# Order of the up/gate loop in a fused attention and gated feed-forward layer: weight block outermost instead of token block outermost

## What is computed

```python
def _L0_ffn_ref(x, w_gate, w_up, w_down):      # w_* are int32, scaled by 1/127
    gate = jnp.einsum('bsd,hd->bsh', x, wg)
    up = jnp.einsum('bsd,hd->bsh', x, wu)
    h = jax.nn.silu(gate) * up
    return jnp.einsum('bsh,dh->bsd', h, wd)

x = L0_attn_x                                  # (4, 4096, 1024) float32
x = x + _layernorm(_L0_attn_ref(_layernorm(x), W_spin, b_spin, W_global, W_J, beta))
x = x + _layernorm(_L0_ffn_ref(_layernorm(x), w_gate, w_up, w_down))
```

## Time and profile before

| what | value |
| --- | --- |
| median of 2 runs | 1491.61 us (1490.85 to 1492.37) |
| the profiled execution, its own time | 1483.44 us |
| its span on the slowest core (core 3) | 1480.8 us |
| spans of the 8 cores | 1467.2 to 1480.8 us |
| share of the span in which TensorE was busy | 81% |
| bytes read from and written to HBM | 167.81 MB, 25.17 MB |

### The profile page before, as it was taken

One profiled execution on the slowest core, in us unless ns is written; L12 is line 12 of the kernel. 1 busy time (PEld: TensorE's weight loads), 2 busy tenths in 40 slices (PEclk: granted clock), 3 DMA queues, 4 the chain that ended last, 5 costly groups with the idle time before them and its releaser, 6 DMA issues.

```text
span 1480.2 us, 14639 instructions; the slowest of 8 cores (1467.2 to 1480.8 us)
## 1 busy us (share of the span) xinstructions
PE 1201.1 (81%) x5274; PEld 512.8 (35%) x5274; DVE 376.8 (25%) x608; ACT 217.8 (15%) x338; POOL 200.6 (14%) x236
## 2 busy tenths in 40 slices
PE   0888887699999999999960777787787666699997
PEld 0233332234444444444420333333333222244443
DVE  2243344101121121121124322332332111123443
ACT  0111112111122122122120111111112100000000
POOL 0011110000000000000010333333343433200000
PEclk9999999999999999999985898999999988899999
DMA  9756557551223233223129999999999999923332
GB/s 191 141 137 134 119 139 192 96 97 43 50 53 72 48 56 72 45 58 72 36 69 251 113 166 169 144 182 163 143 159 146 148 120 131 146 62 114 91 109 85
DMA packets 380150, 168.77 MB, mean 114 GB/s; under 512 B 354480, under 2 KB 354480, under 8 KB 380080
## 3 DMA queue, kind: packets, MB, share of 16 engines
q0 software_dynamic: 207504, 67.13, 43.5%
q1 hardware_dynamic: 102688, 79.74, 22.0%
q10 hardware_dynamic: 69888, 20.98, 7.2%
HBM read 167.81 MB, written 25.17 MB: 130 GB/s over the span
## 4 chain that ended last, share of the span: by engine, by line
PE 64%; DMA 27%; DVE 3%; issue 2%; POOL 1%; ACT 1%; SPq 1%; ACTq 1%; DVEq 0%; POOLq 0%
DMA wu_sb<-wuT 19%; PE ps_q L544 15%; PE ps_pv L651 15%; PE ps_d L1102 11%; PE ps_s L257 6%; PE ps_g L955 6%; DMA xnT_sb<-xn_bf 5%; PE ps_u L967 5%; PE ps_e L306 3%; DMA xs<-x 1%; PE ps_s L253 1%; POOL wg_sb L932 1%; DMA xn2T<-xn_bf 1%; PE ps_pv L428 1%; DMA x_sc<-x_buf 1%
## 5 line engine op out<-in xcount | busy, mean ns | idle before, releaser
L955 PE MATMUL ps_g<-xn2T,wg_sb 128*128 128x512 bf16 x768 | 196.4, 402 | 179.1 <-DMA wu_sb<-wuT 122.7
L544 PE MATMUL ps_q<-s_FM,ebuf 128*128 128x512 bf16 x1024 | 226.6, 382 | 9.0 <-DMA ebuf<-e_sc 9.0
L651 PE MATMUL ps_pv<-s_tok,PT_sb 128*128 128x512 bf16 x1024 | 225.3, 381 | 0.9 <-DVE g_bc L494 0.9
L932 POOL DMA_DIRECT2D wg_sb<-wgT x96 | 84.6, 881 | 802.0 <-DMA attn_sc<-attn_wb 477.9
L967 PE MATMUL ps_u<-xn2T,wu_sb 128*128 128x512 bf16 x768 | 187.3, 388 | 0.0
L955 PEld LDWEIGHTS ps_g<-xn2T,wg_sb 128*128 128x128 bf16 x768 | 74.2, 101 | 290.4 <-issue 219.0
L1102 PE MATMUL ps_d<-wdT_sb,h_act 128*128 128x512 bf16 x768 | 165.9, 379 | 1.1 <-DVE h_act L990 1.1
L990 DVE SCALAR_TENSOR_TENSOR h_act<-silu_b,ps_u 128x512 bf16<-128x512 f32 x96 | 65.2, 686 | 332.2 <-PE ps_u L967 308.1
L544 PEld LDWEIGHTS ps_q<-s_FM,ebuf 128*128 128x128 bf16 x1024 | 100.3, 98 | 132.6 <-issue 14.0
L651 PEld LDWEIGHTS ps_pv<-s_tok,PT_sb 128*128 128x128 bf16 x1024 | 100.7, 98 | 122.9 <-issue 3.4
L257 PE MATMUL ps_s<-wspT_sb,xnT_sb 128*128 128x512 bf16 x512 | 135.0, 411 | 0.0
(11 more groups left out here) (67 smaller groups left out, 436.6 us busy)
## 6 DMA issues: line engine op xcount, KB each, us to landing
xs<-x SPq DMA_DIRECT2D x24, 1024.0 KB, 6.4
wg_sb<-wgT POOLq DMA_DIRECT2D x96, 256.0 KB, 9.5
wu_sb<-wuT POOLq DMA_DIRECT2D x96, 256.0 KB, 13.1
x_sc<-x_buf SPq DMA_DIRECT2D x16, 512.0 KB, 8.0
xs<-x_sc SPq DMA_DIRECT2D x16, 512.0 KB, 4.5
out<-out_b SPq DMA_DIRECT2D x16, 512.0 KB, 5.3
wdT_sb<-wdT POOLq DMA_DIRECT2D x4, 1536.0 KB, 19.6
e_sc<-e_stage POOLq DMA_DIRECT2D x32, 128.0 KB, 2.4
```

Of the source, the lines that this page charges most:

```text
L544: i = t.matmul(ps_q[:, slot, half * 512:(half + 1) * 512], ebuf[:, qt % 2, j, :], s_FM[:, j, qi * 1024 + half * 512: qi * 1024 + (half + 1 ...
L651: i = t.matmul(ps_pv2[:, nb * 512:(nb + 1) * 512], PT_sb[:, par, cb * P:(cb + 1) * P], s_tok[:, cb, nb * 512:(nb + 1) * 512], start=(cb == ...
L932: gp.dma_start(out=wg_sb[:, par], in_=wgT_r[:, :, hb * P:(hb + 1) * P]).then_inc(sem.h, 16)
L955: i = t.matmul(ps_g[:, slot, :], wg_sb[:, par, j, :], xn2T[:, j, tb * 512:(tb + 1) * 512], start=(j == 0), stop=(j == KC - 1))
```

## The change

The four token blocks become the inner loop and the 24 hidden blocks the outer one, so that a pair of weight blocks is loaded once and serves four groups; there are 24 loads instead of 96. For this all four token blocks must be ready, so groups 1 to 3 of the preparation are put ahead of the loop in the order of the program. w_down's first part is issued on GpSimd's queue before the loop, behind the first three weight loads, and waits there until the whole preparation is over. Place in PSUM and slot of silu's buffer are now given by the token block.

```diff
--- before.py
+++ after.py
@@ -997,58 +997,59 @@
             slot_rd[("u", slot)] = sv.n
             sb_rd[sbs] = sv.n
 
+        for g in range(1, 4):
+            for t_i in range(4 * g, 4 * g + 4):
+                l2_grpA(t_i)
+            l2_sqrt(g)
+            l2_grpB(g)
+        s_flush()
+        l2_done = dict(sv=rec[("xn2", NT_OWN - 1)],
+                       ss=rec[("sq3g", NT_OWN // 4 - 1)],
+                       dt0=dtm[0].n, dt1=dtm[1].n,
+                       da0=da[0].n, da1=da[1].n,
+                       tr=[(s_, s_.n) for s_ in (dtp[0], dtp[1])])
+        ctx2.close()
+        wdT_sb = ctx34.enter_context(
+            nc.sbuf_tensor("wdT_sb", [P, HC, D], BF16, side="right"))
+
+        def wdT_part(i4):
+            def f(gp, i4=i4):
+                if i4 == 0:
+                    gp.wait_ge(sv.h, l2_done["sv"])
+                    gp.wait_ge(ss.h, l2_done["ss"])
+                    gp.wait_ge(dtm[0].h, l2_done["dt0"])
+                    gp.wait_ge(dtm[1].h, l2_done["dt1"])
+                    gp.wait_ge(da[0].h, l2_done["da0"])
+                    gp.wait_ge(da[1].h, l2_done["da1"])
+                    for s_, v_ in l2_done["tr"]:
+                        gp.wait_ge(s_.h, v_)
+                gp.dma_start(out=wdT_sb[:, i4 * 6:(i4 + 1) * 6, :],
+                             in_=wdT_r[:, i4 * 6:(i4 + 1) * 6, :]
+                             ).then_inc(dwF.h, 16)
+            block.gpsimd(f)
+            dwF.n += 16
+
         ffn_wload(0)
         ffn_wload(1)
         ffn_wload(2)
-        wdT_sb = None
-        for p in range(4):
-            if p == 3:
-                s_flush()
-                l2_done = dict(sv=rec[("xn2", NT_OWN - 1)],
-                               ss=rec[("sq3g", NT_OWN // 4 - 1)],
-                               dt0=dtm[0].n, dt1=dtm[1].n,
-                               da0=da[0].n, da1=da[1].n,
-                               tr=[(s_, s_.n) for s_ in (dtp[0], dtp[1])])
-                ctx2.close()
-                wdT_sb = ctx34.enter_context(
-                    nc.sbuf_tensor("wdT_sb", [P, HC, D], BF16, side="right"))
-
-                def wdT_part(i4):
-                    def f(gp, i4=i4):
-                        if i4 == 0:
-                            gp.wait_ge(sv.h, l2_done["sv"])
-                            gp.wait_ge(ss.h, l2_done["ss"])
-                            gp.wait_ge(dtm[0].h, l2_done["dt0"])
-                            gp.wait_ge(dtm[1].h, l2_done["dt1"])
-                            gp.wait_ge(da[0].h, l2_done["da0"])
-                            gp.wait_ge(da[1].h, l2_done["da1"])
-                            for s_, v_ in l2_done["tr"]:
-                                gp.wait_ge(s_.h, v_)
-                        gp.dma_start(out=wdT_sb[:, i4 * 6:(i4 + 1) * 6, :],
-                                     in_=wdT_r[:, i4 * 6:(i4 + 1) * 6, :]
-                                     ).then_inc(dwF.h, 16)
-                    block.gpsimd(f)
-                    dwF.n += 16
-            for hb in range(HC):
-                k = p * HC + hb
-                ffn_group(k, hb, p, hb % 4, hb % 4,
-                          w4=(rec[("xtr4", p)] if hb == 0 else None))
-                if k + 3 < 4 * HC:
-                    ffn_wload(k + 3)
-                if p < 3:
-                    if hb in (1, 5, 9, 13):
-                        l2_grpA(4 * (p + 1) + (hb - 1) // 4)
-                    if hb == 17:
-                        l2_sqrt(p + 1)
-                        l2_grpB(p + 1)
-                else:
-                    if hb in (0, 6, 12, 18):
-                        wdT_part(hb // 6)
+        wdT_part(0)
+        for hb in range(HC):
+            for tb in range(4):
+                ffn_group(hb, hb, tb, tb, tb,
+                          w4=(rec[("xtr4", tb)] if hb == 0 else None))
+            if hb + 3 < HC:
+                ffn_wload(hb + 3)
+            if hb == 6:
+                wdT_part(1)
+            if hb == 12:
+                wdT_part(2)
+            if hb == 18:
+                wdT_part(3)
 
         s_flush()
-        hmul_done = rec[("hmul", 4 * HC - 1, 3)]
-        ffn_done = dict(st=rec[("up_mm", 4 * HC - 1, 3)],
-                        ss=rec[("silu", 4 * HC - 1, 3)], sv=hmul_done)
+        hmul_done = rec[("hmul", HC - 1, 3)]
+        ffn_done = dict(st=rec[("up_mm", HC - 1, 3)],
+                        ss=rec[("silu", HC - 1, 3)], sv=hmul_done)
         ctx23.close()
         ctxPS.close()
```

## The result

The changed kernel takes 1402.22 us (median of 11 runs, 1399.59 to 1403.71), the kernel before 1486.79 us (median of nine runs, 1481.21 to 1492.37, with those shown earlier). The ratio is 0.9431, 95% interval 0.9411 to 0.9451: 5.7% faster. In some executions the cores of one die show a lower granted clock and take some per cent longer; times and ratios from here on are of the others, and the rows of the one profile that was of such an execution (half the loads) are of a core of its other die. The profiled execution of the changed kernel took 1403.1 us with a span of 1401.1 us on core 2, its slowest; before, 1483.44 us on core 3.

A forecast was written before the change was run, and what follows sets the result against it. Bound: weight transfers, 5.26 us a pair against 3.45 us of matmul. Preparation ending at 898.6 plus the loop gave 1221.5 instead of 1304.5; 83 us off 1483.4 is 1400.4, plus 8.2 forecast as 1408 us, range 1385 to 1440.

The forecast's parts named there:

- What bounds the kernel: Up/gate stage: weight transfers at 5.26 us a pair against 3.45 us of matmul; 152 us lost.
- Weight loads at nothing: Up/gate loop: 24 pairs, each serving 13.8 us of matmul, hidden by TensorE's work; cost nothing.
- VectorE free at 813: End of preparation group 0: one weight pair less, 5.3 us, frees VectorE at 813 instead of 818.4.
- The period of a group: Exposed preparation: groups 1 and 2 take 29.3 us each, group 3 takes 27; last transpose at 898.6.
- three waits on transposes forecast at 20 to 30 us each: Sign of being right: TensorE waits three times on preparation transposes, 20 to 30 us each, the last ending near 900.
- The loop: Up/gate loop after the preparation: one cold group of 5.5 us, then 92 of 3.45 us, 317.4 us; end 1221.5.
- The rest: Down projection unchanged at 165.5 us with the same waits before it; stages A and C untouched.
- From the profile to the median: Whole kernel: 8.2 us added to the profiled execution's 1400.4, as the median of runs shown stood above it.
- (a): Rival, fourth hidden block: fourth weight pair late behind w_down's first part, TensorE waits some 25 us; 1434 us, chance 0.06.
- (b): Rival, dense loop: clock falls to 0.83, 66 us more, 1475 us, or some 1483 by the 13/16 rule; chance 0.07.
- (c): Rival, exposed preparation: costs more than the weights did, 78 us a group, kernel 1561 us; decides from 56; chance 0.03.
- (d): Rival, program order: loads stay 96 or preparation stays between groups; held excluded by instruction order, no chance given.

The follow-up runs named there:

- four pairs up front and the second chunk behind: Two passes of two token blocks, 48 loads, four weight pairs loaded up front, preparation writes split, second chunk asked for behind the transposes, against the kernel before: 1343.40 us, ratio 0.9018.
- the two-pass kernel: Changed kernel's loop made two passes of two token blocks, 48 weight pairs, preparation groups 2 and 3 between first-pass matmuls: 1365.0 us, ratio 0.9189 to the kernel before.

## Why the prediction was right, point by point

The forecast was 1408 us with 83 us saved in the profiled execution; measured are 1402.2 us and 1483.4 - 1403.1 = 80.3 us. The mechanism held; that the loop opened within 2 us of the forecast is in part luck, since two terms were off against each other.

**What bounds the kernel: right.** The rate of the weights. A load for every group in the new order brings back 131.7 us of waits; half the loads in the old order take them down to 2.8 us; asking earlier changes little. The bound of 5.26 us a pair measured 4.84 us where nothing but weights and w_down moved.

**Weight loads at nothing: right.** No wait on wu_sb. Landing times of the changed kernel, over all 24 pairs, first w_gate and then w_up:

```profile
DMA to landing us min/median/max: 4.2/4.5/38.7
DMA to landing us min/median/max: 5.0/5.7/41.2
```

The longest are from the crowd at the start. In the loop a pair is there after 5.7 us and needed after 41.

**VectorE free at 813: wrong, 819.4.** I had taken one pair less as 5.3 us less. The third pair's w_up, issued at 777.5, took the 41.2 us of the row above and landed at 818.7, when the transposes of group 0 did. In the kernel before, the fourth pair's w_up, issued at 779.69, took the 39.1 us of the earlier trace rows and landed at 818.8: at the same time. VectorE stood on group 0's transposes for 15.8 us beside four pairs and 17.3 us beside three, and for 7.0 us with all three held back. The term should have been nothing. Why three pairs take as long as four stays open.

**The period of a group, 29.3 and 29.3 and 27 us: 27.2, 28.0 and 26.2.** 4 us too high in sum, which by luck cancels most of the 6.4 us of the term before: 898.6 forecast, 900.7 measured. (Of the three waits on transposes forecast at 20 to 30 us each, the last was 16.6.) But my reason for it was partly wrong. I let two readings lead to 29: the bytes of a group, and the rule of the Trainium skill ("DMA: Bandwidth & Descriptors", Queues, rings and completion order) that descriptors are consumed in ring order on each DMA engine. From it I had concluded that a transpose waits out the chunk ahead of it in its queue. From ScalarE's queue, with nothing ahead of them, VectorE stands as long as before. With the chunk out of the way VectorE stands 2.8 us. So the transfers in flight delayed them, not their place in a ring; in the earlier trace rows the two can't be told apart. Bytes alone were not shown to be the limit either: the DMA engines' share in the two middle groups was 0.74 and 0.80, as these rows of the changed kernel show. But moving the chunk, without a byte less, shortened these groups only to 25.9 and 26.3 us, because its bytes are then waited for in the next group; the 22 us that I had for transposes without a chunk ahead were not reached.

```profile
819.00:846.60 27.60, 6.07 (x16) 2.05 (x16) 17.46 (x27) 0.39 (x1) 0.00 (x0) 0.56 0.74 221
846.60:874.60 28.00, 5.76 (x16) 2.05 (x16) 17.08 (x27) 0.39 (x1) 0.00 (x0) 0.56 0.80 226
```

**The loop: right.** The cold group took 907.01 - 900.74 = 6.3 us (5.5 forecast), the 92 behind it 317.9 us (317.4), 3.455 us each. There is no wait of TensorE on ScalarE or VectorE in it.

**The rest: right.** The down projection begins 1.05 us after the last matmul of the loop, as before, and runs from 1225.93 to 1391.85, 165.9 us (forecast 166).

**From the profile to the median: off by 9 us.** I added the 8.2 us by which the two runs shown stood above the profiled one. With nine runs that is 3.3 us, and the changed kernel's median is 0.9 us below its profiled run. Without the 8.2 the sum was 1400.4, nearer to 1402.2.

**The rivals.** (a) The fourth pair came with time to spare. DMA issues of the changed kernel from 822 to 910 us:

```profile
wdT_sb<-wdT POOLq DMA_DIRECT2D x1, 1536.0 KB, 14.5
wg_sb<-wgT POOLq DMA_DIRECT2D x2, 256.0 KB, 14.0
wu_sb<-wuT POOLq DMA_DIRECT2D x2, 256.0 KB, 14.5
```

Issued at about 902, it landed some 15 us later, together with w_down's part and not behind it, and was needed at 935. (b) The clock held at 1.00 in 305 us of dense matmul on all eight cores, as it had on all eight in the 400 us of attention before. The rule of the Trainium skill ("TensorE: Matmul & The Clock Gate", Seeing it yourself), 13/16 from the third core of a die on, was not seen in the profiled executions before and after, in either dense stage. (c) A group at 28 us stayed at half of the 56 from which it would have decided. (d) The issues of weight pairs were 24.

## What to carry to other kernels

When a stage waits for operands, divide its length by the number of transfers and compare that with the work that each serves: 5.26 against 3.45 us said both that a deeper prefetch would gain little (it gained 0.7%) and that four times the reuse would make the loads vanish. Reuse is only worth buying until the loads are covered: two token blocks a pair was enough, and the preparation that four blocks need up front cost more than the other 24 loads. A preparation that is exposed should be looked at for what is in flight beside its small, urgent transfers; moving one bulk load behind them, or holding back loads that are not yet needed, gained 7 to 8 us each, most of it where the crowd was densest, in the first group.

## What the runs showed of the hardware

- A 256 KB weight block that lands in 4.5 to 5.7 us in the loop took 16.4 us as the first and 41.2 us as the last of six issued within 5 us, beside chunks and x1 writes. The 1 MB loads of x issued at the same time took 8.6 and 14.8 us. Leaving out the last of four pairs did nothing for the transposes beside them (15.8 us of stand with four, 17.3 with three).
- The first transposes of a group made VectorE stand for about 8 us beside a chunk in flight, whether they were issued from the chunk's queue or from another, and 2.8 us without it.
- VectorE's L812 took 0.79 to 0.81 us in all tiles of the exposed preparation of the changed kernel, but 1.20 to 1.22 us in all 12 tiles between matmul groups of the kernel before. Each of these 12 began within 0.2 us after the issue of a weight load on GpSimd had begun. The matmuls beside it are not what matters: with four pairs up front and the second chunk behind, the tile at 827.99 took 0.79 us in the middle of dense matmuls, with no issue on GpSimd. In the two-pass kernel one tile began 0.02 us after the issue; it took 0.81 us, and the issue 1.30 us where others take 0.88. VectorE, then GpSimd, in that kernel:

```profile
867.96 1.21 DVE L812 TENSOR_SCALAR ln_tmp<-ab_buf,mv_all,rs_all 128x1024 f32<-128x1024 bf16 x1
874.87 0.81 DVE L812 TENSOR_SCALAR ln_tmp<-ab_buf,mv_all,rs_all 128x1024 f32<-128x1024 bf16 x1
...
874.85 1.30 POOL L932 DMA_DIRECT2D wg_sb<-wgT  x1 [5.21 <-PE ps_u L967]
```

  Where L812 and the issue L932 overlap in these rows, one of the two is 0.4 us longer. It is 5 us over 12 tiles and was hidden in the kernel before.
- Matmuls of 128x512 went at 3.455 us for 16 for over 300 us without a gap, on eight cores at once, at a granted clock of 1.00.
